# Graph attention and mixture of experts in one kernel: stack transfers of two heads sent complete first, the first units of a batch one slot later

## What is computed

```python
def gnn(x, adj, Wq, Wk, Wv, Wg, bg):          # x: layernorm of the input
    q, k, v = (split_heads(x @ W.T) for W in (Wq, Wk, Wv))      # 8 heads of 32
    scores = einsum('bqhd,bkhd->bhqk', q, k) / sqrt(32)
    attn = softmax(where(adj != 0, scores, -inf))
    c = einsum('bhqk,bkhd->bqhd', attn, v).reshape(b, n, h)
    gate = sigmoid(concatenate([c, x], axis=2) @ Wg.T + bg)
    return gate * x + (1.0 - gate) * c
def ffn(x, router_w, ...):                    # x: layernorm
    w, idx = top_k(softmax(x @ router_w), 2)  # 8 experts, weights made to sum to 1
    # experts: (silu(x @ Wg[e]) * (x @ Wu[e])) @ Wd[e], weighted; plus one shared expert
x = x + gnn(layernorm(x), adj, ...)
x = x + ffn(layernorm(x), ...)
```

## Time and profile before

| | |
|---|---|
| time, median of 3 runs | 1810.76 us (1809.15 to 1811.35) |
| the profiled execution | 1823.27 us, its span 1820.5 us |
| TensorE busy | 1726.1 us, 95% |
| DVE busy | 1279.7 us, 70% |
| ScalarE busy | 1102.4 us, 61% (mostly in the attention phase, up to about 870 us) |
| GpSimd busy | 643.7 us, 35% |

### The profile page before, as it was taken

One profiled execution on the slowest core, in us unless ns is written; L12 is line 12 of the kernel. 1 busy time (PEld: TensorE's weight loads), 2 busy tenths in 40 slices (PEclk: granted clock), 3 DMA queues, 4 the chain that ended last, 5 costly groups with the idle time before them and its releaser, 6 DMA issues. The chain is left out here.

```text
span 1820.5 us, 35931 instructions
## 1 busy us (share of the span) xinstructions
PE 1726.1 (95%) x12469; PEld 1456.1 (80%) x12469; DVE 1279.7 (70%) x3185; ACT 1102.4 (61%) x2509; POOL 643.7 (35%) x479
## 2 busy tenths in 40 slices
PE   5899999999999999999899999899999999999996
PEld 4677787777777777777688888789888989888986
DVE  5677877877777777777455554577778777777773
ACT  4888888988888888888434333234434343443442
POOL 0135544344554444454131000023344433444334
PEclk8999999999999999998999999999999999999999
DMA  5454565555555555554243344365565555565553
GB/s 150 127 158 132 159 174 162 169 153 173 142 151 174 163 164 165 161 156 124 84 137 105 104 152 140 128 202 133 165 168 163 155 160 139 163 174 163 141 142 38
DMA packets 140946, 269.19 MB, mean 148 GB/s; under 512 B 15072, under 2 KB 92256, under 8 KB 135776
## 3 DMA queue, kind: packets, MB, share of 16 engines
q1 hardware_dynamic: 113760, 230.45, 41.1%
q0 software_dynamic: 26592, 35.67, 9.7%
q10 hardware_dynamic: 416, 0.79, 0.2%
HBM read 141.99 MB, written 74.52 MB: 119 GB/s over the span
## 5 line engine op out<-in xcount | busy, mean ns | idle before, releaser
L849 DVE CUSTOM_DVE_ANT_0 pf<-bank,bias_q 128x512 f32<-128x512 f32 x512 | 349.1, 688 | 195.1 <-PE bank L493 179.6
L1202 POOL DMA_INDIRECT out_x<-yb,ix x142 | 247.7, 1745 | 567.7 <-ACT yb L1426 467.5
L1438 ACT ACTIVATE ah<-am 128x512 fp32r<-128x512 f32 (+1 forms) x220 | 133.1, 605 | 440.5 <-DVE am L1506 434.5
L622 ACT ACTIVATE pf<-pf,nmax 128x512 f32<-128x512 f32 x512 | 374.2, 731 | 32.8 <-DVE nmax L849 29.9
L1337 PE MATMUL bank<-xh,wh 128*128 128x512 f32 (+1 forms) x880 | 336.3, 382 | 0.9 <-ACT pt L610 0.9
L1338 PE MATMUL bank<-xl,wh 128*128 128x512 f32 (+1 forms) x880 | 335.7, 381 | 0.0
L1339 PE MATMUL bank<-xh,wl 128*128 128x512 f32 (+1 forms) x880 | 335.1, 381 | 0.0
L503 PE MATMUL bank<-ident,pf 128*128 128x128 f32 x2048 | 314.4, 276 | 21.0 <-ACT pt L610 15.8
L503 PEld LDWEIGHTS bank<-ident,pf 128*128 128x128 f32 x2048 | 252.4, 142 | 81.8 <-issue 34.6
L610 ACT ACTIVATE pt<-bank 128x512 f32<-128x512 f32 x512 | 306.9, 599 | 12.0 <-PE bank L503 10.0
L493 PE MATMUL bank<-stack 96*128 96x512 f32 x512 | 234.8, 459 | 27.3 <-DMA stack<-qk 23.6
(11 more groups left out here) (209 smaller groups left out, 3073.6 us busy)
## 6 DMA issues: line engine op xcount, KB each, us to landing
raw<-in_w_all SPq DMA_DIRECT2D x39, 1536.0 KB, 7.1
stack<-qk SPq DMA_DIRECT2D x378, 128.0 KB, 2.4
xb<-xg_dram SPq DMA_DIRECT2D x32, 520.0 KB
adj_i<-in_adj SPq DMA_DIRECT2D x32, 512.0 KB, 4.7
xn<-in_x SPq DMA_DIRECT2D x16, 512.0 KB, 6.4
xn_dram<-xn SPq DMA_DIRECT2D x16, 512.0 KB
xp<-in_x SPq DMA_DIRECT2D x16, 512.0 KB, 6.6
xnp<-xn_dram SPq DMA_DIRECT2D x16, 512.0 KB, 7.8
```

Of the source, the lines that this page charges most:

```text
L622: act.activation(pf[i][:, :], pf[i][:, :], ACT.Exp, bias=nmax[:, i:i + 1], scale=-1.0, accum_out=den[:, g, tq, j:j + 1]).then_inc(p_exp, 1)
L849: dve.tensor_tensor_reduce(pf[r][:, :], S[p % 2][:, :], bias_q[1 - par][:, tq, :], -SCALE, -3.0 * MASKED, ALU.add, ALU.min, nmax[:, r:r + ...
L1202: pool.indirect_dma_start(out=out, out_offset=bass.IndirectOffsetOnAxis(ap=ix[n % RING][:, i:i + 1], axis=0), in_=yb[s][:, i, :], in_offse ...
L1438: act.activation(ah[s][:, m, 0:cols], am[m % 2][:, 0:cols], ACT.Copy).then_inc(s_ah, 1)
```

## The change

It has two parts. The first changes the order in which SyncE sends the stack transfers of heads 0 to 3 for the next batch. Before: rows 0 and 1 of all four heads, then, after K0's low part, rows 2 of all four. After: rows 0 and 1 of heads 0 and 1, then, after K0's low part, rows 2 of heads 0 and 1, then all rows of head 2 and of head 3. The second part shifts units: L0 from slot 0 to 1, M0 from 1 to 2, Q1, K1, V0 and V1 one slot further each; the second half of V1 now shares slot 10 with C0. With them go `exp` (5 to 6), `choose` (3 to 4), `mark` (4 to 5), `bias0` (4 to 6) and `weigh` (6 to 13). The order of the units stays.

```diff
-UNIT_AT = {"L0": 0, "M0": 1, "Q1": 2, "K1": 4, "V0": 6, "V1": 8, "C0": 10, "C1": 11, "R0": 12, "Z0": 14, "Z1": 15, "Z2": 16,
+UNIT_AT = {"L0": 1, "M0": 2, "Q1": 3, "K1": 5, "V0": 7, "V1": 9, "C0": 10, "C1": 11, "R0": 12, "Z0": 14, "Z1": 15, "Z2": 16,
            "Z3": 17, "P0": 18, "P1": 19, "Q0": 22, "K0": 24, "X0": 29, "X1": 30}
-ACT_AT = {"exp": 5}
-DVE_AT = {"choose": 3, "mark": 4, "weigh": 6, "place": 14, "stat": 12, "var": 12, "bias0": 4, "bias1": 16, "gate": (17, 19),
+ACT_AT = {"exp": 6}
+DVE_AT = {"choose": 4, "mark": 5, "weigh": 13, "place": 14, "stat": 12, "var": 12, "bias0": 6, "bias1": 16, "gate": (17, 19),
...
                         sp.wait_ge(g_hi, hi_index(b, "K0") + 1)
                         sp.nop().then_inc(s_held_sp, 1)
-                        for r in range(GRP):
+                        for r in (0, 1):
                             send_head(sp, r, range(2))
                         sp.wait_ge(g_free, unit(b, "K0") + 1)
-                        for r in range(GRP):
+                        for r in (0, 1):
                             send_head(sp, r, range(2, 3))
+                        for r in (2, 3):
+                            send_head(sp, r)
```

## The result

The changed kernel takes 1805.57 us (median of 20 runs, 1804.01 to 1810.09), the kernel before 1810.32 (20 runs, 1808.29 to 1813.1). The ratio is 0.9976, 95% interval 0.997 to 0.9983: 4.75 us or 0.24% faster. The prediction was 1804.0, range 1799.5 to 1809.5. The profiled execution took 1805.60 us (span 1803.9); that of before was itself 12.5 us over its median, so the two profiles must not be subtracted from each other.

The account below looks back on a forecast made before the run. TensorE, busy 95% of the span, bounds the kernel. Seams 8.8 us won, less V1 0.7 and batch 0 1.3, plus join 0.6 and 0.4, make 7.8; 7 taken off the median 1810.76 gives 1804, range 1799.5 to 1809.5.

Parts of the forecast that it names:

- Head 0 to 2 never late, head 3 the new limit: Seams between batches: heads 0 to 2 land in time; head 3's last transfer can hold slot 3, up to 1 us.
- The growth of the wait for copies: TensorE's wait for ScalarE's copies at L503, 13.7 us before, grows by no more than 3 us in all.
- Even seams, 0.1 each: Seams 4 and 7: slot 4 starts 5.46 us after slot 31's start u, residue 0.34; 0.11 saved each, 0.2 together.
- Uneven seams, 7.55: Twelve seams with long issues or late landings: six save 0.87 us on average (5.2), six 0.39 (2.35).
- Seam 1, 1.0: Seam without logits, TensorE stood 2.27 us: 1.6 us saved at usual matmul times, 1.0 if some are drawn out; 1.0 taken.
- V1, 0.7: V1's copy in DVE's slot 11 costs slot 12 between 0 and 0.1 us a batch; 0.05 taken, 0.7 in fifteen.
- The rival that V1 decides all: V1's copy holds slot 12 in every batch, making the kernel slower: at 0.7 us a batch 1814.3 us; chance 0.08.
- Batch 0, 1.3 lost: Second half of adj_i comes 1.4 us later, DVE's wait grows to about 3.9 us, slot 19's score waits: 1.3 lost.
- The join, 1.0 won: Join with the expert phase: 0.6 us won at the last round's M0, 0.4 before the first expert matmul.
- The rule weighed: Lateness belongs to the place in the order, staying with head 3; were it head 1's own, seams gain about 1.4 us.
- the shift of Q1: Q1 one slot later no longer stands before slot 3; Q1 has slots to spare, nothing is added on TensorE.

Follow-up runs that it names:

- first profile of before: Profiled execution of the unchanged kernel before, span 1820.5 us, 12.5 us over its median; median of the runs 1810.32 us.
- the second: Second profile of the kernel before, no edit: span 1807.6 us, median 1809.51 us.
- the order alone: New order of the stack transfers only, units and steps as in the kernel before: 1799.06 us, ratio 0.9935 to the kernel before; again 1800.74 us, 0.9938.
- the shift alone: Old order of the transfers, units and steps shifted as in the changed kernel: 1811.14 us, ratio 1.0005 to the kernel before.
- the second trial: The changed kernel run once more without any edit: 1806.98 us, ratio 0.9977 to the kernel before.
- with L0 and M0 shifted: New order of the transfers, only L0 and M0 one slot later, Q1 to V1 as before: 1798.51 us, ratio 0.9929 to the kernel before.
- the kernel with Q1 and K1 put back: The changed kernel with Q1 and K1 back at slots 2 and 4, V0 and V1 still shifted: 1804.36 us, ratio 0.9959 to the kernel before.
- the kernel with V0 and V1 put back: The changed kernel with V0 and V1 back at slots 6 and 8: 1810.14 us, ratio 0.9991 to the kernel before.

## Why the prediction came out

The direction, the size and the wait named were right: 7 us forecast, 4.75 measured. But the size is in part luck: two terms came out through the clock and not through what they were reckoned from, and the price of the shift was missed. By steps:

- **Head 0 to 2 never late, head 3 the new limit.** Right. Rows of the changed kernel above: the wait at slot 0 is gone in seams 2 to 15, and what is left stands at slot 3, 0.7 us printed in three places; from start to start it is 1.8 us in six seams. The growth of the wait for copies was put at up to 3 us; it was 2.4 against the first profile of before and 1.1 against the second. That growth comes with the order and not with the shift: the order alone has 16.2 us in that row too, the shift alone 15.1.
- **Even seams, 0.1 each.** Too high: 18.09 against 18.04 to 18.10. Slot 3 came at u + 4.04 and slot 4 at u + 5.57, so the residue was 0.45 and not 0.34, and ate the whole 0.11 (slot 2 with M0 lasts 0.98 where the prediction had 0.93, and it starts 0.08 later). This is the mis-sized term that recurs in every seam.
- **Uneven seams, 7.55.** With the 0.2 of the even ones the forecast for seams 2 to 15 was 7.8; on the first profile they gave 261.86 - 254.93 = 6.9. Against the second, 259.1 - 254.9 = 4.2. The prediction said that long issues and late landings might be that one execution's own; part of it was.
- **Seam 1, 1.0.** It took 18.70 instead of 20.86 and 20.94: 2.2 won. Its scores took 0.47 to 0.50 us each, with none at 0.79; I had counted on some being drawn out. The drawn-out scores of before are the stretch at 0.5 from 75.00 on. With the old order but full clock (shift alone) seam 1 took 19.35, and with the whole change the second trial took 19.15. So of the 2.2 us the order has between 0.2 and 0.7; the rest is the clock, some 1 us, and a ninth transfer that landed 0.5 us later in the kernel before than in the shift alone.
- **V1, 0.7.** Measured 0.09 x 15 = 1.35 us at slot 12, within the bound of 0.1 a batch; 0.07 x 15 = 1.05 us by slot 31. The rival that V1 decides all did not come about.
- **Batch 0, 1.3 lost.** The number fits (28.92 to 30.23) by luck, the reason doesn't: DVE's wait for the adjacency was 2.22 us, not 3.9, and the stretch at 0.5 is what drew the batch out. The second trial of the changed kernel, at full clock, lost nothing. It isn't the shift's price.
- **The join, 1.0 won.** M0 of the last round waited 1.12 instead of 1.70, as predicted, but the waits of the transposes of attention results in the same stretch grew by 0.5. From the last score to the first expert matmul it was 4.82 instead of 5.06, 0.25 and not 0.4 (the printed wait there grew from 0.88 to 0.98; the distance is the sure figure). Together some 0.3.

The sum by the measured terms, against the second profile of before: 4.2 + 2.2 - 1.35 - 1.3 + 0.3 = 4.05 us; the two spans differ by 3.7, and the medians give 4.75.

**The rule weighed** was whether lateness goes with the place in the order. In seam 9 of the changed kernel the ninth transfer was the late one (3.8 us, the last three 2.7 to 2.9), while head 1's low part, now sixth, took 2.3. And the landings from 3.5 to 4.1 us in seam 5 belong to the fourth to sixth transfer in before, in the changed kernel and in the order alone, whichever heads these places carry. That speaks for the place, as the prediction took it, though in seam 9 the first late place moved from the tenth to the ninth. Why those places and not others, no run here shows. The Trainium skill (DMA: Bandwidth & Descriptors, "Queues, rings and completion order") says that a completion signal lands only after the earlier writes of its own DMA engine, and that completions are not first in, first out for the engine that issues them. The trace agrees with the latter: in that seam 9 the tenth landed at u + 2.21, before the ninth at u + 2.56.

**What the prediction did not see** is that its second part gives back more than half of what the first wins. It asked of every moved unit only whether something would be late, found spare room, and costed the shift of Q1 at nothing. But Q1 in front of slot 3 was the cover of head 3's transfer. With Q1 there, slot 3 is due at u + 4.76, and in seams 2 to 15 the twelfth transfer had landed by u + 4.5 in the order alone, in that with L0 and M0 shifted and in the kernel with Q1 and K1 put back, also where an issue was long; only later trials saw it land past u + 4.6, up to 4.82. With Q1 one slot later it is due at u + 4.04, sooner than the twelfth lands in seams 2, 3, 5, 11, 12 and 14 (u + 4.14 to 4.56). Nor is anything won by the earlier slot 3 in an even seam: slot 4 comes at u + 5.57, where with Q1 in slot 2 the same work is done at 4.76 + 0.70 = 5.46.

What each unit's shift costs depends on what stands beside it. By ratios: order alone 0.9935, with L0 and M0 shifted 0.9929, with V0 and V1 shifted as well 0.9959, with Q1 and K1 too 0.9976. The third step, V's, is then 0.3%, the fourth 0.17%. Taken the other way round, Q1 and K1 first, it goes from 0.9929 to 0.9991 and back to 0.9976: there Q1 and K1 cost 0.62% and V's shift wins 0.15%. From first to last score, without batch 0 and its clock, the first way is 1.8 and 2.0 us, the other 3.2 and 0.6; both sum to 3.8. The intervals of 0.9959 and of 0.9991 both touch that of the changed kernel. Shown is thus the price of the two together, 0.47% by ratios. The medians say 8.5 us for it, so more than half is not traced to a place. From the first expert matmul to the end, which the change hardly touches, the profiled executions of all versions took 944.7 to 952.6 us, with no order in it that follows the change. This stays open, and with it the median of the kernel with V0 and V1 put back.

## What to carry to other kernels

Before a unit is moved out of the way of a late transfer, ask which other transfer it was covering: the same unit may delay one score and give another the time to arrive. When a change has two parts that the code lets stand alone, time each: here the first alone is worth 0.65%, both together 0.24%, and the second alone nothing, so neither the sum nor the second part's own trial would have shown it. Take a second profile of the kernel before when its own time lies above the median of the runs, before terms are read from its uneven stretches. And look at the granted clock of a stretch before its length is put down to a wait: here it made 1.2 us in batch 0 and, as an estimate from the runs above, some 1 us in seam 1 look like the work of the change.

## What the runs showed of the hardware

SyncE's twelve equal transfers are even in some seams in every execution (4, 7: 0.6 us apart, 2.3 to 2.4 to land) and uneven in others: up to three in a row take 3.1 to 4.4 us to land, and where they stand early in the row a later issue mostly takes 1.3 to 2.1 us. In seams 5, 8, 11 and 14 the fourth was among them in before, after and the order alone, three programs whose times at that point differ by up to 20 us. The granted clock of TensorE falls to 0.5 in one execution and not in the next of the same kernel: batch 0 of the changed kernel had 3.4 us of it in the first trial and none in the second, though TensorE stood still for 1.23 us in the same place in both. 3.4 us at the lower clock cost 1.2 to 1.6 us there, and 6.8 us cost 3.4 (32.36 against 28.98). An execution under the profiler can also be 0.7% over the median, with TensorE slower in slots 20 to 27 of every batch at full clock and no cause in the trace (12.6 us in the first profile of before, of which 4.9 in 16 places are printed as idle; none in the second).
